# The first six scan units of the next item set beside the last sums, gating, out projection and norm of the item before

## The chip, the core and the metric

The kernel runs on one core of one Trainium2 chip. The metric is the device time of one execution in microseconds (us), as the median of several runs. The engines are TensorE (PE in the rows, with PEld its weight loads), VectorE (DVE), ScalarE (ACT), GpSimd (POOL) and SyncE (SP, here a DMA queue).

## What is computed

Eight items of 256 tokens and 256 features go through one block each. It is an FFN with 32 experts (the six best by a router, plus a shared part), then a Mamba mixer followed by a gated MLP, then the FFN again:

```python
x = x + 0.5 * ffn(layernorm(x))
h = layernorm(x)                               # attn's own input
h = h + mamba_mixer(rmsnorm(h, ln1_w))         # scan over 256 tokens, 512 channels, 16 states
x = x + h + mlp(rmsnorm(h, ln2_w))             # 1024 hidden
x = x + 0.5 * ffn(layernorm(x))

# the mixer's recurrence, for each token
hstate = exp(dt * A) * hstate + (dt * x) * B
y = sum over the 16 states of (hstate * C), + x * D_param, times silu(z), then out_proj
```

Everything is computed in float32 accuracy; the FFN's up and gate weights are split into a high and a low part and multiplied in three matmuls.

## The kernel before

The work is a pipeline over steps `t` = -1 to 9. Step `t` runs the first FFN of item `t` or a later one and the second FFN of an earlier item together, the mixer of item `t - 1`, and the MLP of item `t - 2`. In steps 1 and 3 to 7 the FFN handles two items at once (512 columns, the "full steps"), in the others one (256 columns).

`items_of(t)` writes the order of each step as one list of named pieces, and each engine walks that list and does its part of each piece, waiting on semaphores. So each engine is in order, and the list sets what stands beside what. In a step there are two lists that are merged:

- **heavy**: the MLP's 8 chunks (`gum`: gate and up, `down`), then the FFN's 26 chunks (`g`, `u`: six matmuls each; `by_g`: a VectorE product; `by_u`, `by_comb`: GpSimd products; `down`). The last six pieces (`TAIL`) follow the merge.
- **light**: the mixer. The 32 scan units of the item (`ub`: TensorE spreads B into a bank and VectorE multiplies it by `dtx`; `unit`: VectorE scans, TensorE spreads C, VectorE multiplies by it, GpSimd adds), with `front(1, "own")` (the second half of the projections) and the first norm and routing among the first 16, and `front(0, "next")` (the first half of the next item's projections), the norms before it and another routing among the last 16. Then the item's end: `yz` 3 (gating of the last quarter), `outp` (out projection on TensorE, after which VectorE adds it to `hn` and `res`), and `norm("rms2")`, whose result the next step's first `gum` needs.

`merge` gives each list a length by the table `WEIGHT`, scales both to 1, and sorts. The pieces of the item's end have large weights there, and so has what follows unit 31 (8): the light list is stretched at its end:

```python
    light += merge(unit_items(1), follow, SPACE) if follow else unit_items(1)
    light += [("yz", JC - 1), ("outp",)] + norm("rms2")
```

Step 2 differs: its mixer also does the norms and `front(0, "own")` of its item before unit 0 (`late_front`). Steps 7 and 8 differ too (`own`): after the MLP stands a serial chain, layernorm, router, eight dependent routing pieces and the split of the FFN's input (`hx`), before the first FFN chunk of the step can begin; about two thirds of the first half's units are merged with the MLP and this chain.

Small TensorE results go through three PSUM banks, `side0` to `side2`, in turn. A fill waits until the fill three before it has been used up: the bank of an `ub` is free when its unit has been scanned (line 1271), the bank of a `unit` when it has been multiplied (1277), that of `outp` when both additions (1289, 1290) are done. `near` pulls the closing piece of a bank forward when two other fills have come in between, and `late_order` lets VectorE and GpSimd do some pieces (`unit`: one, `outp`: four, `nm`: three) that many pieces later than the others. The scan writes to a ring of three buffers, which GpSimd's additions (1394, 1397) set free; the last additions of a quarter (1400, 1403) come before its `yz` (1282).

## Time and profile before

| | |
|---|---|
| median of 3 runs | 1793.54 us (1791.44 to 1796.31) |
| profiled execution | 1797.3 us, its span 1795.5 us |
| TensorE, matmuls | 1556.8 us busy (87%) |
| VectorE | 1288.6 us busy (72%) |
| GpSimd | 993.8 us busy (55%) |
| ScalarE | 842.9 us busy (47%) |
| step 2 (one item, late front) | 214.4 us |
| steps 3 to 6 (full) | 198.4, 199.7, 198.4 and 198.9 us |
| step 7 (full, with the serial chain) | 213.1 us |
| step 8 (one item, with the serial chain) | 156.9 us |

A step is taken here from the end of the last FFN `down` matmul of one step to that of the next. The steps follow each other on every engine, so the steps' lengths add up to the span. A busy time is the union of an engine's instructions; TensorE's matmuls overlap, and their busy time holds some of their waiting.

### The profile page before, as it was taken

How to read it: one execution, taken by the hardware profiler on the slowest of the kernel's cores; microseconds unless marked ns; L12 is line 12 of the kernel's file. 1: busy time of each engine (PE TensorE's matmuls, PEld its weight loads, DVE VectorE, ACT ScalarE, POOL GpSimd, SP SyncE). 2: the span in 40 equal slices, each digit the busy share in tenths (PEclk: the TensorE clock that was granted, in tenths of full speed). 3: DMA queues.
4: the chain of work that ended last, by engine and by line, in shares of the span. 5: the costliest groups of instructions: out<-in, count | busy, mean ns of one | idle time of the engine just before them, and what ended most of it. 6: DMA issues, size and time to landing. Idle time of an engine off the chain costs nothing. (4 is left out here: it accounts for less than half of the span.)

```text
span 1795.5 us, 22504 instructions
## 1 busy us (share of the span) xinstructions
PE 1556.8 (87%) x7088; PEld 1136.3 (63%) x7088; DVE 1288.6 (72%) x2085; ACT 842.9 (47%) x1676; POOL 993.8 (55%) x1048
## 2 busy tenths in 40 slices
PE   6878888777788999899998999899985999868979
PEld 5756555655676666666666666666663666647868
DVE  4536995478968878687959887887857776679421
ACT  4434543545624563356534663456433553445323
POOL 2523676345545766376646666476633766348525
PEclk9989999978989999999999999999996999979989
DMA  6863223332332323242333223232321332224434
GB/s 220 318 206 98 78 82 101 96 100 85 101 105 90 115 84 110 70 138 78 111 102 118 83 90 112 85 129 84 105 79 41 123 100 102 82 86 158 145 104 147
DMA packets 72278, 200.25 MB, mean 112 GB/s; under 512 B 9921, under 2 KB 22433, under 8 KB 71777
## 3 DMA queue, kind: packets, MB, share of 16 engines
q1 hardware_dynamic: 63968, 173.65, 29.1%
q0 software_dynamic: 8192, 25.17, 4.8%
q8 instruction: 57, 0.93, 0.2%
q14 instruction: 61, 0.49, 0.1%
HBM read 173.62 MB, written 23.59 MB: 110 GB/s over the span
## 5 line engine op out<-in xcount | busy, mean ns | idle before, releaser
L737 PE MATMUL gub<-x_hi,wr 128*128 128x512 f32 (+1 forms) x1040 | 425.4, 409 | 50.6 <-DVE hid L1107 44.8
L1397 POOL TENSOR_TENSOR ring<-ring 128x512 f32<-128x512 f32 x192 | 253.6, 1321 | 307.4 <-DVE ring L1277 306.2
L1376 POOL TENSOR_TENSOR hid<-hid,u_sb 128x512 f32<-128x512 f32 (+1 forms) x260 | 289.6, 1114 | 236.1 <-ACT u_sb L970 199.0
L818 PE MATMUL acc<-hid,w_down 128*128 128x512 f32 (+1 forms) x1040 | 408.9, 519 | 1.8 <-POOL hid L1376 1.8
L739 PE MATMUL gub<-x_hi,wr 128*128 128x512 f32 (+1 forms) x1040 | 370.8, 357 | 0.0
L738 PE MATMUL gub<-x_lo,wr 128*128 128x512 f32 (+1 forms) x1040 | 370.2, 356 | 0.0
L1271 DVE TENSOR_TENSOR_SCAN ring<-decays,side 128x512 f32<-128x512 f32 x256 | 310.5, 1213 | 28.9 <-ACT decays L1069 24.6
L970 ACT ACTIVATE u_sb<-gub 128x512 f32<-128x512 f32 (+1 forms) x260 | 132.7, 510 | 347.3 <-PE gub L739 346.8
L980 ACT ACTIVATE hid<-gub 128x256 f32<-128x256 f32 (+1 forms) x324 | 156.8, 484 | 278.2 <-PE gub L739 153.7
L1384 POOL TENSOR_TENSOR hid<-hid,weight 128x512 f32<-128x512 f32 (+1 forms) x240 | 272.9, 1137 | 15.8
L737 PEld LDWEIGHTS gub<-x_hi,wr 128*128 128x128 f32 x1040 | 205.4, 197 | 93.6 <-issue 58.1
L818 PEld LDWEIGHTS acc<-hid,w_down 128*128 128x128 f32 x1040 | 189.2, 197 | 97.2 <-issue 80.8
L1069 ACT ACTIVATE decays<-dts,a_neg 128x255 f32<-128x255 f32 x512 | 228.8, 497 | 3.8 <-DVE ring L1271 3.6
L1262 DVE TENSOR_TENSOR side<-dtx,side 128x512 f32<-128x512 f32 x256 | 176.8, 690 | 69.0 <-PE side L912 68.3
L739 PEld LDWEIGHTS gub<-x_hi,wr 128*128 128x128 f32 x1040 | 204.6, 197 | 27.1
L738 PEld LDWEIGHTS gub<-x_lo,wr 128*128 128x128 f32 x1040 | 205.8, 198 | 24.4 <-issue 5.5
L1107 DVE SCALAR_TENSOR_TENSOR hid<-hid,gub 128x512 f32<-128x512 f32 (+1 forms) x260 | 149.0, 573 | 98.3 <-ACT hid L980 98.3
L1277 DVE TENSOR_TENSOR ring<-ring,side 128x512 f32<-128x512 f32 x256 | 176.0, 687 | 59.5 <-PE side L915 36.2
L885 PE MATMUL side<-rn,w_in 128*128 128x256 f32 x448 | 120.4, 417 | 18.7 <-DVE ring L1271 13.5
L912 PE MATMUL side<-bst,sel_b 96*128 96x256 bf16 x512 | 103.7, 285 | 33.9 <-DVE ring L1271 18.1
L915 PE MATMUL side<-cst,sel_c 96*128 96x256 bf16 x512 | 103.9, 286 | 33.2 <-DVE ring L1271 32.7
L779 PE MATMUL gub<-xn_mlp,wm_gu 128*128 128x256 f32 x512 | 122.4, 387 | 0.0
(120 smaller groups left out, 1823.3 us busy)
## 6 DMA issues: line engine op xcount, KB each, us to landing
wr<-w_halves SPq DMA_DIRECT2D x234, 512.0 KB, 3.3
wm_gu<-in_w_mlp POOLq DMA_DIRECT2D x64, 256.0 KB, 3.1
w_halves<-wr SPq DMA_DIRECT2D x26, 512.0 KB, 4.9
wm_down<-in_w_mlp POOLq DMA_DIRECT2D x64, 128.0 KB, 2.6
w_raw<-in_w_gu SPq DMA_DIRECT2D x26, 256.0 KB, 4.3
rows<-parts SPq DMA_DIRECT2D x16, 384.0 KB, 2.3
cst<-rows SPq DMA_DIRECT2D x48, 128.0 KB, 2.6
xin<-in_x SPq DMA_DIRECT2D x8, 256.0 KB, 2.9
```

Source lines behind the costliest of these rows:

```text
L737: mm(out, w[:, 0, half, k, :], x_hi[:, k, a:b], start=(k == 0), stop=False)
L738: mm(out, w[:, 0, half, k, :], x_lo[:, k, a:b], start=False, stop=False)
L739: last = mm(out, w[:, 1, half, k, :], x_hi[:, k, a:b], start=False, stop=(k == KC - 1))
L818: last = mm(acc[k][:, a:b], w, h[:, a:b], start=(c == 0), stop=(c == (MLP_CHUNKS if mlp else FFN_CHUNKS) - 1))
L980: A(hid[c % HSLOTS][:, a:b], s.gub_of(it)[:, a:b], ACT.Tanh, scale=0.5).then_inc(sem["tanh_done"], 1)
L1069: A(decay[u % 2][:, h, 1:SEQ], dts[:, j, 1:SEQ], ACT.Exp, scale=a_neg[:, j, n:n + 1]).then_inc(sem["decay"], 1)
L1262: v.tensor_tensor(b, twice(dtx[:, j, :]), b, ALU.mult).then_inc(sem["driven"], 1)
L1271: v.tensor_tensor_scan(w.rearrange("p h s -> p (h s)"), decay[u % 2][:, :, :].rearrange("p h s -> p (h s)"), s.side_of(("ub", u))[:, :], 0 ...
L1277: v.tensor_tensor(w, w, pair(s.side_of(it)), ALU.mult).then_inc(sem["read_out"], 1)
L1376: nc.gpsimd.tensor_tensor(h, h, u_sb[c % USLOTS][:, a:b], ALU.mult).then_inc(sem["hidden"], 1)
L1384: nc.gpsimd.tensor_tensor(h, h, weight[c // 3 % CSLOTS][:, a:b], ALU.mult).then_inc(sem["weighted"], 1)
L1397: add(ysum, ysum, ring[:, u % 3], ALU.add).then_inc(sem["y_sum"], 1)
```

## The change

`LEAD = 6` units of an item are moved from the beginning of its step to the end of the step before. There they are merged, by the table `SPACE`, with the end of the item before (`yz` 3, `outp`, `rms2`). Steps 2 to 7 have such an end; steps 3 to 8 begin with unit 6. In steps 2 to 7 the extra weights of the item's end and after unit 31 are gone; they are kept as `ENDING` for steps 1 and 8, whose end nothing shares. The two additions behind the out projection become a piece of their own, `om`, so that other pieces can stand between; and the units carry their item's number, from which the ring's place and the scan's wait for a free buffer are worked out across items. The number of FFN columns in each step is as it was.

```diff
+LEAD = 6
...
-    "outp": {"side_filled": 1, "mixed": 2},
+    "outp": {"side_filled": 1},
+    "om": {"mixed": 2},
...
+def ring_at(unit):
+
+    return (unit[2] * UNITS + unit[1]) % 3
+
+
+def sums_of(u):
+    return {0: 0, PAIRS - 1: 3}.get(u % PAIRS, 1)
...
-    begin = len(light)
-    light += merge(unit_items(0), front(1, "own") + ln1, SPACE)
-    light += merge(unit_items(1), follow, SPACE) if follow else unit_items(1)
-    light += [("yz", JC - 1), ("outp",)] + norm("rms2")
+    begun = merge(unit_items(t - 1, 0 if late_front else LEAD, UNITS // 2), front(1, "own") + ln1, SPACE)
+    light += begun
+    units = unit_items(t - 1, UNITS // 2, UNITS)
+    light += merge(units, follow, SPACE) if follow else units
+    last = [("yz", JC - 1), ("outp",), ("om",)] + norm("rms2")
+    light += merge(unit_items(t, 0, LEAD), last, SPACE) if next_front else last
+    weight = WEIGHT if next_front else ENDING
...
-        cut = begin + len(unit_items(0) + front(1, "own")) * 2 // 3
-        out = hand + keep + merge(chain, light[:cut], WEIGHT) + merge(ff[:-TAIL], light[cut:], WEIGHT) + ff[-TAIL:]
+        cut = len(begun) * 2 // 3
+        out = hand + keep + merge(chain, light[:cut], weight) + merge(ff[:-TAIL], light[cut:], weight) + ff[-TAIL:]
...
-          "ub": 2, "unit": 2, ("unit", UNITS - 1): 8, "rt1": 1, "yz": 0.4,
-          ("yz", JC - 1): 3, "outp": 3, ("n1", "rms2"): 3, ("n2", "rms2"): 3, ("nm", "rms2"): 2,
+          "ub": 2, "unit": 2, "rt1": 1, "yz": 0.4, "outp": 0.5, "om": 1.6,
...
-         "yz": 0.1}
+         "yz": 0.1, "outp": 4, "om": 2, ("yz", JC - 1): 2, ("n1", "rms2"): 2}
+
+ENDING = {**WEIGHT, ("unit", UNITS - 1, BATCH - 1): 8, ("unit", UNITS - 1, 0): 8, ("yz", JC - 1): 3, "outp": 3, ("n1", "rms2"): 3,
+          ("n2", "rms2"): 3, ("nm", "rms2"): 2}
...
-       "xm": 0, "z": 0, "zm": 0, "dt": 0, "sp": 1, "sp_dt": 0, "sp_x": 0, "y0": 0, "ub": 0, "unit": 1, "rt1": 0, "outp": 4,
+       "xm": 0, "z": 0, "zm": 0, "dt": 0, "sp": 1, "sp_dt": 0, "sp_x": 0, "y0": 0, "ub": 0, "unit": 1, "rt1": 0, "outp": 0, "om": 0,
...
-                    w = ring[:, u % 3, :, :]
-                    dve.wait_ge(sem["decay"], s.count("decay", ("ub", u), 2))
-                    dve.wait_ge(sem["driven"], s.count("driven", ("ub", u), 1))
-                    if u >= 3:
-                        by = u - 3 if (u - 3) % PAIRS else u - 2
-                        dve.wait_ge(sem["y_sum"], s.count("y_sum", ("unit", by), 1))
+                    ub = ("ub",) + it[1:]
+                    w = ring[:, ring_at(it), :, :]
+                    dve.wait_ge(sem["decay"], s.count("decay", ub, 2))
+                    dve.wait_ge(sem["driven"], s.count("driven", ub, 1))
+
+                    free = u - 3 if (u - 3) % PAIRS else u - 2
+                    still = sum(sums_of(x) for x in range(free + 1, u)) + sums_of(free) - 1
+                    if (least := s.count("y_sum", it, 0, back=still)) is not None:
+                        dve.wait_ge(sem["y_sum"], least)
```

What this does to the engines' order is shown at three places. Line numbers of the changed kernel are up to 20 higher (818 is 835 there, 1271 is 1291).

VectorE at the end of step 4, before: from `y0` of the next item (`xs`) over the gating (`yg`) and the additions behind the out projection (`hn`, `res`) to the step's last additions (`x1_next`):

```order
L1253 TENSOR_SCALAR xs<-xs,vecs 128x256 x2
L1282 TENSOR_TENSOR yg<-xs,z2 128x256
L1107 SCALAR_TENSOR_TENSOR hid0<-hid0,gub1 128x512
L1289 SCALAR_TENSOR_TENSOR hn<-side0,hn 128x512
L1290 SCALAR_TENSOR_TENSOR res<-side0,res 128x512
L1107 SCALAR_TENSOR_TENSOR hid1<-hid1,gub0 128x512
L1172 SCALAR_TENSOR_TENSOR xn_mlp<-hn,lnw,rstd 128x256 x2
L1133 SCALAR_TENSOR_TENSOR x1_next<-acc0,x1_next 128x256
```

The same place after, from the gating on (the scan is printed as a SCALAR_TENSOR_TENSOR that writes `ring`):

```order
L1302 TENSOR_TENSOR yg<-xs,z2 128x256
L1291 SCALAR_TENSOR_TENSOR ring<-decays,side0 128x512
L1297 TENSOR_TENSOR ring<-ring,side1 128x512
L1279 TENSOR_TENSOR side0<-dtx,side0 128x512
L1124 SCALAR_TENSOR_TENSOR hid2<-hid2,gub0 128x512
L1291 SCALAR_TENSOR_TENSOR ring<-decays,side0 128x512
L1297 TENSOR_TENSOR ring<-ring,side1 128x512
L1309 SCALAR_TENSOR_TENSOR hn<-side2,hn 128x512
L1310 SCALAR_TENSOR_TENSOR res<-side2,res 128x512
L1279 TENSOR_TENSOR side2<-dtx,side2 128x512
L1124 SCALAR_TENSOR_TENSOR hid3<-hid3,gub2 128x512
L1291 SCALAR_TENSOR_TENSOR ring<-decays,side2 128x512
```

Between the gating and the additions behind the out projection stood one FFN product (`hid`). Now the scans and products of units 0 and 1 stand there, with unit 1's first product (1279) and one `hid`; four more units follow.

TensorE at the same place before, from the last FFN `down` ahead of the out projection (`yg,w_out`):

```order
L818 MATMUL acc0<-hid1,w_down 128x512
L818 MATMUL acc1<-hid1,w_down 128x512
L925 MATMUL side0<-yg,w_out 128x256 x8
L737 MATMUL gub2<-x_hi,wr0 128x512
L738 MATMUL gub2<-x_lo,wr0 128x512
```

And after, from the out projection to the fill that takes its bank, `side2`, again (`bst,sel_b` fills for `ub`, `cst,sel_c` for `unit`):

```order
L942 MATMUL side2<-yg,w_out 128x256 x8
L929 MATMUL side0<-bst,sel_b 128x256 x2
L835 MATMUL acc0<-hid3,w_down 128x512
L835 MATMUL acc1<-hid3,w_down 128x512
L932 MATMUL side1<-cst,sel_c 128x256 x2
L754 MATMUL gub1<-x_hi,wr4 128x512
L755 MATMUL gub1<-x_lo,wr4 128x512
L756 MATMUL gub1<-x_hi,wr4 128x512
L754 MATMUL gub1<-x_hi,wr4 128x512
L755 MATMUL gub1<-x_lo,wr4 128x512
L756 MATMUL gub1<-x_hi,wr4 128x512
L929 MATMUL side2<-bst,sel_b 128x256 x2
```

The out projection's bank used to be taken by nothing in the step's last chunks; now it is wanted again after one `down`, two small fills and one FFN half.

TensorE at the start of step 5, before, from the first `ub` (`wm_gu`, `wm_down` are the MLP, `rn,w_in` and `dtr,w_dt` the projections of `front(1)`):

```order
L912 MATMUL side2<-bst,sel_b 128x256 x2
L885 MATMUL side0<-rn,w_in 128x256 x4
L779 MATMUL gub0<-xn_mlp,wm_gu0 128x256 x4
L915 MATMUL side1<-cst,sel_c 128x256 x2
L896 MATMUL side2<-dtr,w_dt 128x256 x2
L912 MATMUL side0<-bst,sel_b 128x256 x2
L818 MATMUL acc0<-hid1,wm_down1 128x256
L818 MATMUL acc1<-hid1,wm_down1 128x256
L915 MATMUL side1<-cst,sel_c 128x256 x2
```

And after:

```order
L929 MATMUL side2<-bst,sel_b 128x256 x2
L902 MATMUL side0<-rn,w_in 128x256 x4
L796 MATMUL gub0<-xn_mlp,wm_gu0 128x256 x4
L913 MATMUL side1<-dtr,w_dt 128x256 x2
L932 MATMUL side2<-cst,sel_c 128x256 x2
L835 MATMUL acc0<-hid1,wm_down1 128x256
L835 MATMUL acc1<-hid1,wm_down1 128x256
L929 MATMUL side0<-bst,sel_b 128x256 x2
```

The `dt` projection moved ahead of the first `unit` fill and out of the bank of the step's first `ub`; the `unit` fill has that bank now. By the end of the MLP part (the eighth `down`) TensorE has filled for units 6 to 10 instead of units 0 to 5 and the `ub` of 6.

## Rows read from the trace of the kernel before

**Rows 1.** The page's busy times, us and share of the span

```profile
PE 1556.8 (87%) x7088; PEld 1136.3 (63%) x7088; DVE 1288.6 (72%) x2085; ACT 842.9 (47%) x1676; POOL 993.8 (55%) x1048
```

**Rows 2.** Busy us by stretch: steps 2, 3, 4, 6, 7 and 8

```profile
core 0: us, PE busy (x) PEld busy (x) DVE busy (x) ACT busy (x) POOL busy (x), PEclk, DMA share, GB/s
313.30:527.70 214.40, 161.26 (x831) 132.89 (x829) 163.55 (x272) 104.72 (x218) 95.49 (x118) 0.87 0.31 98
527.70:726.10 198.40, 184.56 (x783) 126.28 (x781) 159.12 (x248) 101.28 (x191) 121.90 (x118) 0.99 0.30 98
726.10:925.80 199.70, 187.71 (x784) 128.25 (x782) 158.71 (x250) 101.39 (x191) 121.45 (x118) 0.97 0.31 100
1124.20:1323.10 198.90, 182.29 (x767) 123.87 (x764) 155.66 (x227) 97.79 (x185) 122.10 (x118) 0.99 0.31 99
1323.10:1536.20 213.10, 187.43 (x766) 127.85 (x764) 152.10 (x227) 97.66 (x185) 121.37 (x118) 0.94 0.28 91
1536.20:1693.10 156.90, 124.50 (x715) 103.60 (x715) 121.40 (x199) 67.35 (x158) 90.37 (x118) 0.89 0.36 117
```

**Rows 3.** The same for step 4's MLP part, its FFN body, its tail

```profile
726.10:766.40 40.30, 33.08 (x145) 26.13 (x143) 31.66 (x57) 15.00 (x32) 13.38 (x25) 0.88 0.21 65
766.40:906.00 139.60, 135.59 (x574) 90.03 (x572) 119.49 (x185) 79.45 (x149) 100.31 (x89) 1.00 0.35 113
906.00:925.80 19.80, 19.04 (x69) 12.09 (x68) 7.56 (x10) 6.93 (x10) 7.76 (x6) 1.00 0.24 79
```

**Rows 4.** Waits in step 4's MLP part: waiter, awaited, us in total, times, longest

```profile
PE side L885 <- DVE ring L1271: 3.4, 1, 3.4
...
PE side L896 <- DVE ring L1271: 2.4, 1, 2.4
...
PE side L915 <- DVE ring L1271: 1.3, 1, 1.3
```

**Rows 5.** Four lines' instructions: ns min/median/max, first and last start in us

```profile
L1262 DVE TENSOR_TENSOR side<-dtx,side x256: 675/691/697, 164.2 to 1670.7; 128x512 f32<-128x512 f32 x128
...
L1271 DVE TENSOR_TENSOR_SCAN ring<-decays,side x256: 1201/1212/1222, 165.0 to 1671.7; 128x512 f32<-128x512 f32 x128
...
L1277 DVE TENSOR_TENSOR ring<-ring,side x256: 686/687/691, 169.0 to 1673.0; 128x512 f32<-128x512 f32 x128
...
L1282 DVE TENSOR_TENSOR yg<-xs,z x32: 410/420/1511, 218.7 to 1677.4; 128x256 f32<-128x256 f32 x32
```

**Rows 6.** Timeline of PE, end of step 4: start, us, instruction, idle before

```profile
910.16 3.72 PE L925 MATMUL side<-yg,w_out 128*128 128x256 f32 x16 [0.76 <-DVE yg L1282]
...
913.53 0.58 PE L737 MATMUL gub<-x_hi,wr 128*128 128x512 f32 x1
...
916.46 1.13 PE L843 MATMUL side<-sq,mean_w 128*128 128x256 f32 x4
...
920.53 5.31 PE L818 MATMUL acc<-hid,w_down 128*128 128x512 f32 x12
```

**Rows 7.** The same of DVE, the addition behind the out projection

```profile
913.92 0.69 DVE L1289 SCALAR_TENSOR_TENSOR hn<-side,hn 128x512 f32<-128x512 f32 x1 [3.21 <-PE side L925]
```

**Rows 8.** Busy us by stretch: step 2's second half and its tail

```profile
393.00:513.00 120.00, 90.21 (x499) 73.29 (x498) 111.25 (x177) 61.85 (x136) 64.93 (x69) 0.89 0.30 99
513.00:527.70 14.70, 12.15 (x58) 10.35 (x59) 4.89 (x10) 4.91 (x8) 3.48 (x5) 0.88 0.30 96
```

**Rows 9.** The same for three parts of step 7, two of step 8

```profile
1323.10:1358.10 35.00, 27.75 (x141) 21.89 (x138) 29.75 (x54) 15.37 (x33) 14.12 (x25) 1.00 0.23 67
1358.10:1386.10 28.00, 11.34 (x40) 7.38 (x40) 20.41 (x45) 9.40 (x18) 9.68 (x17) 0.61 0.17 52
1386.10:1536.20 150.10, 148.34 (x587) 98.57 (x586) 101.94 (x130) 72.89 (x135) 97.57 (x76) 0.98 0.31 104
...
1572.60:1599.90 27.30, 11.47 (x41) 7.57 (x41) 19.91 (x45) 10.25 (x19) 10.07 (x17) 0.63 0.15 44
1599.90:1674.00 74.10, 64.44 (x434) 55.72 (x433) 67.73 (x96) 35.36 (x94) 56.65 (x64) 0.96 0.49 160
```

More of the change, by code:

```diff
@@ L153, in routing, with unit_items @@
     return [("rt1", call)] + [("rq", call, i) for i in range(len(ROUTE))]
-def unit_items(half):
+def unit_items(item, begin, end):
     out = []
-    for u in range(half * UNITS // 2, (half + 1) * UNITS // 2):
+    for u in range(begin, end):
         j, p = u // PAIRS, u % PAIRS
-        out += [("ub", u), ("unit", u)]
+        out += [("ub", u, item), ("unit", u, item)]
         out += [("yz", j - 1)] if p == 2 and j else []
@@ L186 @@
 FILLS = ("n1", "n2", "rt1", "rt2", "z", "x", "split", "dt", "ub", "unit", "outp")
-ENDS = {"ub": "unit", "z": "zm", "split": "sr", "n1": "nc"}
+ENDS = {"ub": "unit", "outp": "om", "z": "zm", "split": "sr", "n1": "nc"}
 def near(items):
@@ L253, in items_of @@
     if not mlp:
-        out = hand + keep + merge(ff[:-TAIL], light, WEIGHT) + ahead + ff[-TAIL:]
+        out = hand + keep + merge(ff[:-TAIL], light, weight) + ahead + ff[-TAIL:]
     elif own:
         chain = mlp_items() + ahead + norm("ln2a") + routing("f1") + [("rt2", "f1"), ("hx", "f1")]
-        cut = begin + len(unit_items(0) + front(1, "own")) * 2 // 3
-        out = hand + keep + merge(chain, light[:cut], WEIGHT) + merge(ff[:-TAIL], light[cut:], WEIGHT) + ff[-TAIL:]
+        cut = len(begun) * 2 // 3
+        out = hand + keep + merge(chain, light[:cut], weight) + merge(ff[:-TAIL], light[cut:], weight) + ff[-TAIL:]
     else:
         heavy = mlp_items() + ahead + ff
-        out = hand + heavy[:6] + keep + merge(heavy[6:-TAIL], light, WEIGHT) + heavy[-TAIL:]
+        out = hand + heavy[:6] + keep + merge(heavy[6:-TAIL], light, weight) + heavy[-TAIL:]
     out = near(after(out, turn, *turns))
@@ L265, in items_of @@
         at = out.index
-        assert at(("shift",)) < at(("n1", "lnA")) and at(("ub", UNITS // 2)) < at(("split", 0, "next"))
+        assert at(("shift",)) < at(("n1", "lnA")) and at(("ub", UNITS // 2, t - 1)) < at(("split", 0, "next"))
         assert at(("yz", 1)) < min(at(("xc", 0, "next", 0)), at(("z", 0, "next")))
@@ L395 @@
 }
-ENDED_BY = {"g": "by_g", "ub": "unit", "z": "zm", "split": "sr", "n1": "nc"}
+ENDED_BY = {"g": "by_g", "ub": "unit", "outp": "om", "z": "zm", "split": "sr", "n1": "nc"}
 BANKS = {"side": SIDES, "gub": GUBS}
@@ L990, in do @@
                     else:
-                        act.wait_ge(sem["mixed"], s.count("mixed", ("outp",), 1))
+                        act.wait_ge(sem["mixed"], s.count("mixed", ("om",), 1))
                     A(sq[:], src[:], ACT.Square).then_inc(sem["squared"], 1)
@@ L1279, in do @@
                     j = it[1]
-                    dve.wait_ge(sem["y_sum"], s.count("y_sum", ("unit", PAIRS * j + PAIRS - 1), 3))
+                    dve.wait_ge(sem["y_sum"], s.count("y_sum", ("unit", PAIRS * j + PAIRS - 1, s.t() - 1), 3))
                     dve.wait_ge(sem["z_done"], s.count("z_done", it, 0))
                     v.tensor_tensor(yg[:, j], y[:, j], z2[:, j], ALU.mult).then_inc(sem["y_gated"], 1)
-                elif kind == "outp":
-                    dve.wait_ge(sem["side_filled"], s.count("side_filled", it, 1))
+                elif kind == "om":
+                    dve.wait_ge(sem["side_filled"], s.count("side_filled", ("outp",), 1))
                     dve.wait_ge(sem["r_base"], s.count("r_base", ("r0",), 1))
                     dve.wait_ge(sem["carried"], s.count("carried", ("carry",), 1))
-                    b = pair(s.side_of(it))
+                    b = pair(s.side_of(("outp",)))
                     v.scalar_tensor_tensor(hn[:], b, 0.5, hn[:], ALU.mult, ALU.add).then_inc(sem["mixed"], 1)
@@ L1393, in do @@
                             pool.wait_ge(sem["y_sum"], least)
-                        add(ysum, ring[:, (u - 1) % 3], ring[:, u % 3], ALU.add).then_inc(sem["y_sum"], 1)
+                        add(ysum, ring[:, ring_at(("unit", u - 1, it[2]))], ring[:, ring_at(it)], ALU.add).then_inc(sem["y_sum"], 1)
                     else:
                         pool.wait_ge(sem["y_sum"], s.count("y_sum", it, 0))
-                        add(ysum, ysum, ring[:, u % 3], ALU.add).then_inc(sem["y_sum"], 1)
+                        add(ysum, ysum, ring[:, ring_at(it)], ALU.add).then_inc(sem["y_sum"], 1)
                     if p == PAIRS - 1:
```

2 lines of the change are left out of this document (1 added, 1 removed).

## The prediction

> **What bounds the kernel now.** Begin with the page's busy times: the matmuls take 87% of the span and VectorE 72% [rows 1]. Neither number says which engine ends a wait in a given stretch, so the next view is the busy time by step [rows 2]. The full steps are TensorE's: steps 3 and 4 have TensorE busy for 184.6 and 187.7 us of 198.4 and 199.7, VectorE for 159. Step 2 and step 8 are different. In step 2 TensorE is busy for only 161.3 us of 214.4, in step 8 for 124.5 of 156.9, and both have VectorE at 163.6 and 121.4.
>
> Then cut a full step into three [rows 3]. Step 4's last 19.8 us are the item's end: TensorE is busy for 19.0 of them, VectorE for 7.6. This is the hole into which the change puts units. But TensorE is full there, so filling it gives nothing by itself. What can be gained is where TensorE waits, and that is the MLP part: 40.3 us with TensorE busy for 33.1, at a granted clock of 0.88, while the 139.6 us of FFN body have 135.6 busy at 1.00. The waits of that part name three fills that waited for a scan, 3.4, 2.4 and 1.3 us [rows 4]; they are the whole 7.2 us of idle time. So the chain there is TensorE, fill, VectorE's scan, next fill; less scan work in it should help.
>
> In step 2's second half VectorE is busy for 111.3 of 120.0 us, and for only 4.9 of the last 14.7 [rows 8]. Steps 7 and 8 have the serial routing chain: in step 7 the 35.0 us of MLP and 28.0 of chain hold 27.8 and 11.3 us of matmuls and 29.8 and 20.4 us of VectorE, and the FFN part after them is TensorE's (148.3 of 150.1). In step 8 the FFN part is VectorE's: 67.7 of 74.1 us [rows 9].
>
> **The price of a unit.** On VectorE 0.69 + 1.21 + 0.69 = 2.59 us [rows 5], so the six lead units are 15.5 us of VectorE's time. No unit is added or removed in all; each step from 3 to 7 gets six at its end and loses six at its start, step 2 only gets, step 8 only loses. The counts of DMAs and of SyncE's waits don't change; the DMAs that bring B and C for unit 0 are issued some three FFN chunks ahead of it as now placed, and a chunk takes over 5 us, so I cost them at nothing (if that cover were gone, one landing would stand in the open in each of six steps).
>
> **Step 2.** 15.5 us of VectorE work comes in. The tail has 14.7 - 4.9 = 9.8 us of idle VectorE time [rows 8], and I let 8 of it be filled, since part of it lies before the first unit can start or behind the last. The rest lengthens the step: +7.5 us. Bounds: +5.7 (all filled) and +15.5 (none).
>
> **Steps 3 to 5.** In the MLP part TensorE now fills for units 6 to 10 instead of units 0 to 5 and the first product of unit 6. On VectorE this is 5 x 2.59 = 13.0 instead of 6 x 2.59 + 0.69 = 16.2 us, so 3.2 less. In their place two more pieces of the projections' second half come forward, but to the part's end, behind what TensorE waits for there. Beside it, the `dt` projection, which waited 2.4 us for the first scan [rows 4], has a free bank now; the next fill waits for the same scan instead, so only `dt`'s own matmuls are won, some 0.5 us. Sum: -3.7.
>
> At the tail something new is queued. The third lead unit's first fill takes the out projection's bank, `side2`, and must wait for both additions behind it. From the out projection's end TensorE has one `down` (5.31 / 12 x 4 = 1.8 us), one FFN half ((916.46 - 913.53) / 2 = 1.5) and two small fills (0.4 by my estimate) to do, 3.7 in all [rows 6]. VectorE has unit 1's first product, an FFN product of that kind, the scan, the product and the two additions: 0.69 + 0.7 + 1.21 + 0.69 + 2 x 0.69 = 4.7 us [rows 5, 7]. So TensorE stops for about 1 us (with a little for the order, 1.2), and behind it in its queue stand the last FFN chunks. VectorE's own wait for the out projection, 3.2 us now [rows 7], is filled by unit 0, which helps nobody. Net -2.5 us a step, -7.5 for three. Bounds for a step: -7.2 (all idle time of the MLP part gone) and +3 (nothing gained there, three times the tail stop).
>
> **Step 6.** The same, with a little more slack in it (16.6 us without a matmul against 12.0 in step 4, [rows 2]): -3.
>
> **Step 7.** Before the FFN's first chunk VectorE had ten whole units to do, now six: 4 x 2.59 = 10.4 us less in 63.0 us. But VectorE was already idle for 12.9 of them [rows 9], waiting for the chain of small steps, so I count half: -5. The FFN part is TensorE's and gets the fills of five more units: 20 matmuls, at most 0.23 each by the out projection's records [rows 6], so 0 to 4.6, and I take +2. Net -3.
>
> **Step 8.** The same -5 at the start (27.3 us of chain with 19.9 of VectorE, [rows 9]). In the part where VectorE is the limit one unit fewer remains, -2.6, and I round to -3. Net -8.
>
> **Steps 1 and 9** keep their content; in step 1 the additions only move by a place or two: 0.
>
> Sum: +7.5 - 7.5 - 3 - 3 - 8 = **-14 us**. Against the profiled execution's 1797.3 that is 1783.3; the median of the runs is 3.8 us lower, so 1793.5 - 14 = 1779.5.
>
> **A rule weighed against the trace.** The gating (1282) stands between the last sum and the out projection, and it takes 0.41 us at least, 0.42 at the median, but 1.51 at the longest, while the three instructions of a unit never vary by more than 0.02 us [rows 5]. The Trainium skill, SBUF — State Buffer, "SBUF: two separate sides", says that VectorE and GpSimd share one port pair under an exclusive lock, taken by a VectorE instruction with two SBUF inputs, and that the loser blocks for a whole instruction of the other. The rows agree: the gating has two SBUF inputs, the unit's instructions take one of theirs from PSUM. By this rule the units themselves cost their 2.59 us beside any GpSimd work. But GpSimd gets their additions in the tail, and the gating could more often meet one.
>
> **The rivals.**
> - *More is won* (1760). The waits of the MLP part go altogether, and the clock with them: 7.2 us idle and a clock of 0.88 in 40.3 us [rows 3]. Another 5 us in each of steps 3 to 6: -34. For it: all of the idle time there is waiting for scans. Against it: the first unit of the step still meets the same chain of fill, product, scan.
> - *The units only change places* (1793). The full steps stay as they are, since TensorE is busy for 94% of them and VectorE's hole was never in the way; step 2 costs its 7.5 and step 8 gives its 8. For it: the tail's 19.0 of 19.8 us. Against it: the 7.2 us.
> - *The gating is blocked in the tail* (1786). 1.51 - 0.41 = 1.1 us in each of the six tails, +6.6: 1793.5 - 14 + 6.6. For it: the longest 1282. Against it: the median is the free value, beside a GpSimd that is busy for 122 of 200 us. It is the lock rule's case.
> - *Slower: TensorE stops in the tail* (1800 and more). The last sum, gating, out projection, additions and the next fill of `side2` are one chain through three engines, with units now queued ahead of its VectorE pieces. Each microsecond costs six times. I have 1.2 in the sum; with s instead the sum is -14 + 6 (s - 1.2), which is nothing at s = 3.5 and +6.4 at 4.6, a stop as long as all of VectorE's work in that piece. For it: the fill really is behind both additions. Against it: TensorE's 3.7 us of other work ahead of it.
>
> **How the numbers follow.** About 0.3% (5.4 us) is what a measurement of this kernel can tell. Chances: forecast 0.50 (1771 to 1787), more 0.17, change of places 0.12, gating 0.08, slower 0.13. The predicted time is the forecast's, 1779.5. The range leaves out the slower case and a little of "more": 1761 to 1795. Faster by over 0.3% (under 1788.2): 0.50 + 0.17 + most of the gating's, 0.06 = 0.73. Within 0.3%: 0.14. Slower: 0.13.
>
> **What would show it.** Step 2 some 7.5 us longer with VectorE busy over 170 us, and its tail no longer empty; the MLP part of steps 3 to 5 near 37 us with the waits for 1291 (the scan) under 4 us; in the tail one wait of a `side` fill for `res` (1310) of about 1 us; step 7 near 210 and step 8 near 149 us. The prediction is wrong if the full steps don't get shorter, if the MLP part keeps its 40 us, or if the tail grows beyond 21 us. It is too timid if the granted clock in the MLP part rises to 1.00.

## The result, and the profile after

The changed kernel takes 1802.8 us (median of 4 runs, 1801.5 to 1805.2), where the kernel before took 1793.3 beside it: a ratio of 1.0053, 95% interval 1.0035 to 1.0071. It is slower by 0.5%. The forecast was 14 us faster and its range ended at 1795.

The page's busy times (first line below) hardly differ from [rows 1]: no work was added. The second fence has the busy times of steps 2, 3, 4, 6, 7 and 8, columns as in [rows 2].

```profile
PE 1555.1 (86%) x7088; PEld 1136.0 (63%) x7088; DVE 1292.4 (72%) x2085; ACT 843.6 (47%) x1676; POOL 991.2 (55%) x1048
```

```profile
309.40:540.10 230.70, 168.09 (x853) 137.40 (x852) 177.53 (x289) 109.69 (x230) 100.16 (x123) 0.86 0.28 91
540.10:744.90 204.80, 188.56 (x784) 128.87 (x783) 160.88 (x248) 101.79 (x191) 121.20 (x118) 0.97 0.29 94
744.90:945.80 200.90, 184.67 (x783) 125.95 (x782) 160.95 (x250) 101.79 (x191) 121.51 (x118) 0.99 0.31 99
1147.30:1347.00 199.70, 183.77 (x767) 125.53 (x765) 152.60 (x227) 96.52 (x185) 122.53 (x118) 0.97 0.30 99
1347.00:1553.70 206.70, 188.03 (x765) 128.81 (x764) 152.61 (x227) 97.49 (x185) 120.95 (x118) 0.93 0.29 94
1553.70:1696.70 143.00, 116.81 (x692) 99.57 (x691) 106.52 (x181) 62.75 (x146) 84.69 (x113) 0.92 0.39 128
```

Against [rows 2], step by step: step 2 is 16.3 us longer, steps 3, 4 and 5 together 10.6, step 6 0.8; step 7 is 6.4 shorter, step 8 13.9. Steps 0, 1 and 9 differ by -3.0 together. That is the span's +4.5. In step 2 VectorE is busy 14.0 us more (163.6 to 177.5) and the step is 16.3 longer: none of the idle time that VectorE had there was filled. The step is as long as before up to the start of the out projection (202.4 us against 201.3); from there to the step's end it went from 13.2 to 28.3 us, and VectorE's idle time there from 9.8 to 11.0 (before, then after):

```profile
514.55:527.70 13.15, 12.15 (x58) 10.35 (x59) 3.34 (x7) 4.91 (x8) 2.01 (x3) 0.87 0.33 107
511.83:540.10 28.27, 21.16 (x97) 16.97 (x98) 17.28 (x24) 8.95 (x18) 10.37 (x11) 0.80 0.22 70
```

The next fence cuts step 4 into MLP part, FFN body and last 34.9 us, to be held against [rows 3], and adds the last 35.1 us of step 2.

```profile
744.90:779.50 34.60, 28.53 (x141) 23.15 (x140) 28.72 (x54) 14.85 (x31) 13.16 (x25) 1.00 0.24 76
779.50:910.90 131.40, 125.42 (x522) 83.68 (x520) 109.71 (x168) 73.74 (x137) 88.86 (x78) 0.99 0.34 112
910.90:945.80 34.90, 30.72 (x122) 19.12 (x122) 22.52 (x30) 13.20 (x24) 19.49 (x16) 1.00 0.23 76
505.00:540.10 35.10, 22.27 (x105) 17.86 (x106) 23.91 (x35) 10.23 (x22) 14.08 (x15) 0.82 0.22 71
```

The MLP part went from 40.3 to 34.6 us. Everything behind it in the step went from 159.4 to 166.3. The gain of the MLP part is mostly not the one that was forecast: its waits for the scan fell only from 7.1 us [rows 4] to 5.9, and the rest is that TensorE was busy for 28.5 us instead of 33.1, with four matmuls fewer and at a granted clock of 1.00 instead of 0.88. In step 3 the clock of that part went the other way, from 0.96 to 0.90, and the part only from 39.5 to 38.4 us. The waits behind it are among TensorE's waits of the whole of step 4 (waiter, awaited, us in total, times, longest):

```profile
PE side L860 <- ACT sq L1009: 4.3, 1, 4.3
PE side L932 <- DVE ring L1291: 2.5, 3, 1.7
PE side L902 <- DVE ring L1291: 2.3, 1, 2.3
PE side L942 <- DVE yg L1302: 1.8, 1, 1.8
PE side L929 <- DVE ring L1291: 1.4, 1, 1.4
PE acc L835 <- POOL hid L1396: 1.2, 1, 1.2
PE side L929 <- DVE res L1310: 1.2, 1, 1.2
```

Only the waits for the scan (1291) and the old wait for the gating (1302, 0.76 us in [rows 6]) have a counterpart before. Three are new: 4.3 us for the squares of a norm (the first of the FFN part) at 51 us into the step, 1.2 us for the additions behind the out projection, and 1.2 us for a GpSimd product in the step's last piece. The timeline of the trace shows these, and the larger ones of step 2's tail (start, us, instruction, idle before it and what ended it):

```profile
505.86 0.39 PE L932 MATMUL side<-cst,sel_c 96*128 96x256 bf16 x2 [1.18 <-DVE ring L1291]
511.83 6.25 PE L942 MATMUL side<-yg,w_out 128*128 128x256 f32 x16 [4.86 <-DVE yg L1302]
522.38 0.39 PE L929 MATMUL side<-bst,sel_b 96*128 96x256 bf16 x2 [3.00 <-DVE res L1310]
538.01 2.07 PE L835 MATMUL acc<-hid,w_down 128*128 128x256 f32 x4 [4.11 <-POOL hid L1396]
...
796.24 1.06 PE L860 MATMUL side<-sq,mean_w 128*128 128x256 f32 x3 [4.28 <-ACT sq L1009]
...
914.45 3.72 PE L942 MATMUL side<-yg,w_out 128*128 128x256 f32 x16 [1.75 <-DVE yg L1302]
...
922.89 0.39 PE L929 MATMUL side<-bst,sel_b 96*128 96x256 bf16 x2 [1.20 <-DVE res L1310]
...
943.85 1.98 PE L835 MATMUL acc<-hid,w_down 128*128 128x512 f32 x4 [1.23 <-POOL hid L1396]
```

Three things are to be read there. In step 2's tail the stops add up to 13.2 us; but the step's tail before had 3.84 us of waiting for the gating and 1.00 for the GpSimd product already, so what is new is 1.0 for the gating, 3.0 for the additions, 3.1 for GpSimd and the first 1.2. The norm that is waited for stood 65 us into step 4 before (791.54) and nothing waited for it; the merge now puts it at 51. By then VectorE has 11 us less work behind it, but it is wanted 14 us earlier, and from 778.65 to the instruction that feeds the squares (794.84) VectorE goes from one instruction to the next (step 4 from its start to that norm, before and after):

```profile
726.10:791.50 65.40, 57.98 (x255) 43.56 (x253) 55.23 (x90) 29.05 (x60) 35.51 (x51) 0.92 0.36 112
744.90:796.20 51.30, 40.99 (x198) 32.18 (x196) 44.23 (x75) 22.38 (x46) 26.59 (x44) 1.00 0.36 111
```

And the out projection starts 31.4 us before the end of step 4 (914.45 against 945.8), where it used to start 15.6 us before it (910.16 in [rows 6], end 925.8): with six units merged beside it, the whole of the item's own work has to be done earlier in the step.

The last wait is a queue of GpSimd. Its timeline at the end of step 4:

```profile
941.31 1.26 POOL L1417 TENSOR_TENSOR ring<-ring 128x512 f32<-128x512 f32 x1 [3.71 <-DVE ring L1297]
942.53 1.26 POOL L1396 TENSOR_TENSOR hid<-hid,u_sb 128x512 f32<-128x512 f32 x1
```

GpSimd stands idle for 3.71 us until unit 5's product is there, adds it, and only then makes the product that the last `down` waits for. The addition is ahead of it in GpSimd's order; e5 below tests whether it is what holds the product up.

### The profile page after: what moved, and what is told of

It reads as the page before. It is cut to its first block and busy times, and to the rows that moved or that the text cites. A ratio compares the mean times of both kernels' runs of the same rounds, so it can differ in the third digit from the quotient of the medians.

```text
span 1800.0 us, 22495 instructions
## 1 busy us (share of the span) xinstructions
PE 1555.1 (86%) x7088; PEld 1136.0 (63%) x7088; DVE 1292.4 (72%) x2085; ACT 843.6 (47%) x1676; POOL 991.2 (55%) x1048
## 5 line engine op out<-in xcount | busy, mean ns | idle before, releaser
L1404 POOL TENSOR_TENSOR hid<-hid,weight 128x512 f32<-128x512 f32 (+1 forms) x240 | 269.0, 1121 | 14.8
L1086 ACT ACTIVATE decays<-dts,a_neg 128x255 f32<-128x255 f32 x512 | 228.9, 497 | 6.1 <-DVE ring L1291 6.0
L756 PEld LDWEIGHTS gub<-x_hi,wr 128*128 128x128 f32 x1040 | 204.3, 196 | 27.9
```

The lines of the kernel that those rows point to most:

```text
L756: last = mm(out, w[:, 1, half, k, :], x_hi[:, k, a:b], start=False, stop=(k == KC - 1))
L1086: A(decay[u % 2][:, h, 1:SEQ], dts[:, j, 1:SEQ], ACT.Exp, scale=a_neg[:, j, n:n + 1]).then_inc(sem["decay"], 1)
L1404: nc.gpsimd.tensor_tensor(h, h, weight[c // 3 % CSLOTS][:, a:b], ALU.mult).then_inc(sem["weighted"], 1)
```

## The experiments

All run on one core, each timed beside the kernel before; each ratio is to that. "Gives" is a step that starts with unit 6, "receives" one that has the next item's first units at its end.

| kernel | what differs from the changed kernel | us | ratio, 95% |
|---|---|---|---|
| e1 | step 2 doesn't receive | 1792.9 | 0.9994 [0.9983, 1.0004] |
| e2 | only step 7 receives | 1784.2 | 0.9953 [0.9937, 0.9969] |
| e3 | no step receives | 1795.4 | 1.0009 [0.9998, 1.0020] |
| e4 | variance and routing fills of `ln1` later | 1801.8 | 1.0039 [1.0025, 1.0053] |
| e5 | unit 5 behind GpSimd's last product | 1794.2 | 0.9998 [0.9987, 1.0008] |
| e6 | e5, and all leads behind the out projection | 1813.4 | 1.0111 [1.0095, 1.0127] |
| e7 | e5, light work spaced by VectorE time | 1803.1 | 1.0058 [1.0042, 1.0074] |
| e8 | three units instead of six | 1805.3 | 1.0069 [1.0050, 1.0088] |
| e9 | e2, additions at the out projection in steps that don't receive | 1787.0 | 0.9957 [0.9941, 0.9974] |
| e10 | e9 with seven units | 1779.7 | 0.9916 [0.9895, 0.9937] |
| e11 | as e9, but only step 2 receives | 1813.0 | 1.0100 [1.0078, 1.0122] |
| e12 | as e9, but steps 6 and 7 receive | 1781.1 | 0.9934 [0.9911, 0.9956] |
| e13 | e7, one VectorE product moved | 1800.6 | 1.0040 [1.0026, 1.0053] |
| e14 | e11, the same product moved | 1811.8 | 1.0099 [1.0081, 1.0117] |
| e15 | e12 with seven units | 1774.5 | 0.9898 [0.9883, 0.9913] |
| e16 | e12 with six and seven units | 1776.5 | 0.9898 [0.9885, 0.9911] |

**Who pays and who gains: e1, e2, e3.** One table of leads (here e1's; `{7: 6}` in e2, `{}` in e3) replaces the constant:

```diff
-LEAD = 6
+LEADS = {i: 6 for i in range(3, 8)}
...
-    light += merge(unit_items(t, 0, LEAD), last, SPACE) if next_front else last
-    weight = WEIGHT if next_front else ENDING
+    leads = unit_items(t, 0, LEADS.get(t, 0))
+    light += merge(leads, last, SPACE) if leads else last
+    weight = WEIGHT if leads else ENDING
```

> Step 2 keeps all its work; the leads begin with item 3, in step 3's tail, so that step 3 holds 38 units and steps 4 to 8 begin with unit 6. Theory A (the change lost in step 2, which has no room for six units, and a few us at each tail): step 2 returns from 230.7 to about 214 us, step 3 to about 203 (from 204.8), the others stay, so about 1786 us. Theory B (VectorE's work is the limit wherever it stands): the 15.5 us reappear in step 3, which goes to 215 or more, about 1799 us.

> Leads for the last item alone, in step 7's tail; all steps before it as in the kernel before. Theory A (each step that only receives six units pays some 16 us, each that only gives wins some 14, and a step that does both is unchanged): step 7 rises from 213.1 to 225 or more, since it receives and doesn't give, step 8 falls from 156.9 to 143, the sum is 1793 to 1797 us. Theory B (a full step with a VectorE hole in its tail takes six units for nearly nothing, and the loss was step 2's alone): step 7 stays under 218, the sum is 1785 us or less.

> No leads anywhere, the large weights at every item's end, but the additions behind the out projection still a piece of their own, which VectorE meets directly instead of four pieces late. If only the moved units matter: 1793 us as before, within 0.3%. If the separate additions cost or give something by themselves (TensorE or VectorE waiting at the item's end): up to 2 us a step, 1783 to 1805 us.

In e1 step 2 is back at 213.1 us, but step 3, which now receives and doesn't give, takes 215.8, 17.3 more than before. Its busy times, and its longest waits of TensorE:

```profile
519.40:735.20 215.80, 192.39 (x809) 131.03 (x807) 176.68 (x266) 106.27 (x203) 127.56 (x123) 0.97 0.27 90
```

```profile
PE side L933 <- DVE ring L1292: 5.3, 2, 4.7
PE gub L755 <- DVE hid L1125: 3.9, 3, 1.7
PE side L943 <- DVE yg L1303: 3.6, 1, 3.6
```

The total, 1792.9, lies between the two theories, and step 3 is as theory B had it: the price belongs to whichever step receives without giving. Against the changed kernel e1 has step 2 17.6 us shorter and step 3 11.0 longer, and is 10 us faster in the median. e2 moves the price to step 7: 216.0 us, only 2.9 more than before, and step 8 takes 143.9, 13 less. In e3, without any leads, the new separate piece for the additions alone changes nothing that can be measured.

**GpSimd's queue: e5.**

```diff
+    if next_front:
+        out.remove(("unit", LEAD - 1, t))
+        out.insert(out.index(("by_u", "ff", FFN_CHUNKS - 1)) + 1, ("unit", LEAD - 1, t))
     out = near(after(out, turn, *turns))
```

> The changed kernel, but unit 5 of the next item stands behind the step's last GpSimd product, so that its addition no longer lies ahead of that product in GpSimd's queue. If the queue is the cause of the wait of the last downs (4.1 us in step 2, 1.2 in the full steps): 4 us less in step 2 and 1 in each full step, 8 us in all, about 1795 us. If the last product is late for another reason: no change, 1803 us.

The time falls from 1802.8 to 1794.2, which is that of the kernel before. In step 2 the edit changes GpSimd's order alone; in steps 3 to 6 TensorE's too. The wait of 4.1 us at the end of step 2 is 0.7, and step 2 is 3.2 us shorter (227.5); the 1.2 us at the end of the full steps are gone. Step 3 is 5.0 us shorter: 1.5 at its end and 3.6 in its MLP part. Its first 24 matmuls took 7.4 us in the changed kernel, right behind the stop of 4.1, where those of step 4 took 5.4; the granted clock up to the end of the first `down` was 0.75, and it is 1.00 in e5. Steps 4 and 5 are no shorter in the profiles (201.2 and 201.1 us against 200.9 and 201.4), so what the 1.2 us of a full step are worth by themselves is not shown. One piece in the wrong place of one queue was thus worth most of the change's loss (8.6 of 9.5 us); without it the change is worth nothing.

**The order in the tail and in the start: e4, e6, e7.**

In e4, in steps 3 to 5 (the condition holds in these alone):

```diff
+        for it, behind in ((("n2", "ln1"), ("down", "ff", 0)), (("rt1", "f1"), ("down", "ff", 1))):
+            out.remove(it)
+            out.insert(out.index(behind) + 1, it)
```

In e6, with e5's edit:

```diff
-    light += merge(unit_items(t, 0, LEAD), last, SPACE) if next_front else last
+    light += last[:2] + merge(unit_items(t, 0, LEAD), last[2:], SPACE) if next_front else last
```

In e7, with e5's edit, weights for steps 3 to 7 that follow VectorE's time for each piece:

```diff
+EVEN = {**WEIGHT, "ub": 1, "unit": 1.6, "xc": 2.6, "sp": 2.0, "sp_dt": 1.9, "sp_x": 1.0, "y0": 1.8, "sr": 0.6, "rq": 0.7}
```

> The changed kernel, but in steps 3 to 5 the variance matmul of ln1 stands one FFN half and one down later, and the router matmul behind the next down. Theory A (the 4.3 us wait for the square is a cost of the order): it goes to about 1 us in three steps, 8 to 10 us less, about 1793 us. Theory B (VectorE is behind after the MLP part, and TensorE meets it somewhere): the wait moves to the next fill or gate, less than 3 us won, 1800 to 1803 us.

> The kernel with unit 5 behind GpSimd's last product (1794.2 us), and with all six lead units behind the out projection, so that VectorE's first lead product is not ahead of the gating and two units are not ahead of the additions. Theory A (the tail's waits for the gating, 1.8 us, and for the additions, 1.2, come from what is queued ahead of them, and are worth their size): 1.5 to 3 us less in each of steps 2 to 7, so 1777 to 1785 us. Theory B (VectorE's order only decides where TensorE meets it): under 1 us a step, 1789 to 1794 us.

> The kernel with unit 5 behind GpSimd's last product (1794.2 us), and in steps 3 to 7 the weights of the merge changed so that the light list is spaced by VectorE's time (units less, convolution and first product more): some 2 us of VectorE's work move from the first six FFN chunks and the MLP part to later ones. If TensorE's 4.3 us wait at the variance matmul of ln1 is VectorE's backlog at the start of the step: 2 us less in each of steps 3 to 5 and about as much in 6 and 7, 1784 to 1788 us. If the backlog isn't the cause: 1793 to 1796 us.

e4 took the wait of 4.3 us for the squares away, and the waits for the FFN product `hid` went from 0.9 to 4.0: the same lateness of VectorE, met by another reader; nothing was gained that can be told. In e6 the wait for the gating rose from 1.8 to 3.7 us in steps 3 to 5 and the total by 19 us over e5 (8 of them in step 7): that the waits of the tail come from the units queued ahead of the gating was wrong. In e7 the waits for `hid` rose to 6.3 us a step and the total by 9 over e5: that the light work was spaced badly for VectorE was wrong as I had it.

**Fewer units: e8** (`LEAD = 3`).

> The changed kernel with three lead units instead of six (and GpSimd's queue as in the changed kernel). If all costs and gains go with the number of units: half of the way from 1793.3 to 1802.8, 1798 us; step 2 about 222 us, step 8 about 150. If the tail's waits come with the first lead unit (its queueing ahead of the gating, the out projection's bank and the last GpSimd product): step 2 stays above 224, 1800 to 1806 us.

Neither theory holds. Step 2 takes 214.0 us: three units do fit into the hole. But steps 3 to 5 take 204.2 to 205.3 us, 7.6 more together than with six, while step 6 is 3 us shorter (196.4), and step 8 only loses 4.0. So the cost of a full step doesn't go with the number of units; the places into which the pieces fall count for 2 to 3 us a step.

**Giving and receiving priced apart: e9, e11, e12, e10, e15, e16.** In these the weight of `om` in `ENDING` is 0, so steps that neither give nor receive have the order of before.

> Leads for the last item alone (step 7 receives, step 8 gives), and in the other steps both additions stand at the out projection as in the kernel before, so steps 1 to 6 have its order. Theory (the total is what the receiving step pays less what the last giving step wins, and nothing else): step 7 about 215 us (+2 to +3 against before), step 8 about 143 (-13 to -14), total 1782 to 1784, ratio 0.994. If e2's ratio owed something to its changed places of the additions in steps 1 to 6, this one is not better than 1788; if these places cost e2 something (the separate additions with no leads seemed to cost 2 us a step in 3 to 5), this one is under 1781.

> Leads for item 2 alone: step 2 receives six units, step 3 gives and receives none, all other steps have the order of before. This prices what a full step wins when it only gives. Theory A (a full step is TensorE's, and VectorE's load sets its start, so a step that only gives has 15.5 us less for VectorE and loses the waits of its MLP part: 7.2 us of idle and the lower clock): step 3 at 190 to 193 us against 198.5, step 2 at 228 to 231, total +8 to +11, about 1803. Theory B (a full step wins nothing by giving, since TensorE sets it): step 3 at 197 to 199, total +14 to +16, about 1808.

> Leads for the last two items: step 6 only receives, step 7 receives and gives, step 8 only gives; steps 1 to 5 as before. Theory (each step that does both is about as long as before, so the cost moves to whichever step only receives): step 7 at 207 (-6), step 8 at 143 (-14), step 6 +11 to +17 since it is a full step whose VectorE has only its tail free; total 1784 to 1790. Rival (step 6 has more room than a full step: 16.6 us without a matmul): step 6 +5 or less, total 1779 or less, better than e9.

| step | neither | receives | gives | both |
|---|---|---|---|---|
| 2 | 214.4 | 228.9 (e11) | | |
| 3 | 198.4 | 215.8 (e1) | 201.8 (e11), 198.9 (e14, below) | 199.8 to 204.8 |
| 6 | 198.9 | 206.3 (e12) | | 199.2 to 200.2 |
| 7 | 213.1 | 216.6 (e9) | | 206.6 (e12) |
| 8 | 156.9 | | 144.8 (e9), 142.5 (e12) | |

A full step wins nothing by giving six units away: in e11 step 3 is 3.4 us longer than before, though its MLP part shrank from 39.5 us to 34.2 (538.5 to 572.7 in its trace). Theory A of that run fell. Of theory B the outcome holds, with a loss on top (1813 us instead of 1808), but not its reason: TensorE stands idle for 15.9 us of that step, and for 13.8 before, so it is not TensorE's work that fills it; the waits move from the MLP part to later places. A step that receives pays 14.5 us at step 2, 17.3 at step 3, 7.4 at step 6 and 3.5 at step 7. e9's total is 3 us above what was expected, with step 7 at 216.6 and step 8 at 144.8; in e12 step 6's price lies between what its theory and its rival had. Only steps 7 and 8, which have the serial chain, win by giving: 10 and 12 to 14 us. The total is the price of the first step that receives and what the full steps behind it lose (0 to 6 us each), less these two. That is why leads for all items come out at nothing or worse, and leads for the last two are 12 us faster.

> As the kernel of e9 (leads for the last item alone), with seven leads instead of six. Theory (step 7's FFN part has room on VectorE: 102 of 150 us busy): step 7 within 1 us of e9's, step 8 one more unit shorter, 141 to 142, so 1 to 2 us under e9's time. Rival (six fill the room, TensorE sets that part and gets four more small matmuls, about 1 us): the same as e9 within 1 us. If the time is above e9's by 2 us or more, the seventh unit meets the step's last FFN chunks as unit 5 met GpSimd's queue.

> Leads for the last two items as in e12, with seven units in both instead of six. Theory (step 7 and 8 win with each unit more, since step 8 went from 144.8 to 137.5 with the seventh; step 6 only receives and has VectorE room in its tail for about six): step 6 208 to 210, step 7 205 to 207, step 8 137 to 138, total 1774 to 1779. Rival (the seventh unit in a full step meets GpSimd's queue or a full TensorE): step 6 above 212 or step 7 above 209, total 1781 or more.

> As e12 (leads for the last two items), with six units in step 6 and seven in step 7. Theory (the seventh unit's gain is in step 8 alone, 142.5 to about 137.5, and costs step 7 about 2): total 1776 to 1779. Rival: step 8's seventh unit won by chance of its order, and the total stays at 1780 to 1783.

The seventh unit pays more than I expected (e10 is 7.3 us under e9 in the median, expected were 1 to 2): step 8 falls to 137.5 us in all three. The rows of e15 are steps 6, 7 and 8:

```profile
1122.70:1328.80 206.10, 187.43 (x796) 125.97 (x793) 172.97 (x248) 102.99 (x199) 129.56 (x124) 0.98 0.30 96
1328.80:1535.60 206.80, 187.47 (x766) 127.69 (x764) 151.52 (x228) 97.27 (x185) 121.22 (x118) 0.93 0.29 94
1535.60:1673.00 137.40, 117.49 (x687) 100.86 (x686) 101.91 (x177) 62.19 (x144) 82.43 (x112) 0.89 0.42 133
```

e15 is the fastest kernel of this study, 1774.5 us, 18 us under the kernel before (16 to 21). e16 can't be told from it.

**VectorE locked out: e13, e14.** The 6.3 us of waiting for `hid` in e7 are in each of steps 3 to 5 a stop of 4.44 us (last row) and small ones. VectorE's timeline before it, and GpSimd's:

```profile
785.76 0.69 DVE L1301 TENSOR_TENSOR ring<-ring,side 128x512 f32<-128x512 f32 x1
786.37 0.68 DVE L1128 SCALAR_TENSOR_TENSOR hid<-hid,gub 128x512 f32<-128x512 f32 x1
786.97 5.27 DVE L1270 TENSOR_TENSOR dtx<-dts,xs 128x512 f32<-128x512 f32 x1
792.27 1.23 DVE L1274 TENSOR_SCALAR xs<-xs,vecs 128x256 f32<-128x256 f32 x1
...
786.71 1.29 POOL L1400 TENSOR_TENSOR hid<-hid,u_sb 128x512 f32<-128x512 f32 x1
787.96 1.28 POOL L1421 TENSOR_TENSOR ring<-ring 128x512 f32<-128x512 f32 x1
789.20 1.26 POOL L1408 TENSOR_TENSOR hid<-hid,weight 128x512 f32<-128x512 f32 x1
790.43 1.25 POOL L1400 TENSOR_TENSOR hid<-hid,u_sb 128x512 f32<-128x512 f32 x1
791.76 1.60 POOL L1408 TENSOR_TENSOR hid<-hid,weight 128x512 f32<-128x512 f32 x1
...
794.51 0.77 PE L758 MATMUL gub<-x_hi,wr 128*128 128x512 f32 x1 [4.44 <-DVE hid L1128]
```

The product of `dts` and `xs`, both in SBUF, takes 5.27 us where its kind takes 0.68 at the median. It begins while GpSimd is in the first of four instructions that follow each other without a pause, and ends 0.5 us after GpSimd's first pause. In e11's step 3 the same product takes 5.05 us, and TensorE waits 4.84 us behind it. Both kernels put it at the same place, behind unit 11. e13 and e14 put it, with the pair of `xs` products behind it, behind unit 13:

```diff
+        moved = [("sp_x", 1, "own"), ("y0", 1, "own")]
+        out = [it for it in out if it not in moved]
+        at13 = out.index(("unit", 13, t - 1)) + 1
+        out[at13:at13] = moved
```

> As e7 (spaced-out order), but in steps 3, 4 and 5 the piece sp_x (one VectorE product, dtx from dts and xs, both in SBUF) and the y0 behind it stand two units later, away from GpSimd's run of four back-to-back instructions. Theory (VectorE is locked out by that run: 5.27 us instead of 0.68): the instruction is back under 2.1 us, the wait for hid falls by 3 to 4.6 us, and each of steps 3 to 5 is 3 to 4.6 us shorter, 9 to 14 in all, so 1789 to 1794 against e7's 1803. Rival (VectorE's backlog at the step's start is the cause, the long instruction only lies in it): the wait appears at another fill and the total stays at 1801 to 1804.

> As e11 (leads for item 2 alone), but in step 3 sp_x and y0 stand two units later. Theory (the lockout of 4.4 us by GpSimd's run made step 3's wait for hid of 4.8 us): step 3 at 197.5 to 199 us against 201.8, total 1809 to 1810. Rival (backlog): step 3 within 1 us of 201.8.

Its place is cured in both: no instruction of that kind takes over 1.76 us. In e14 step 3 fell from 201.8 to 198.9 us, within what the theory had, though 0.6 us of that lies in the MLP part, ahead of the moved pieces, and one profile can't tell 2.9 us for certain; the total fell by 1.2, which that run can't tell from nothing. In e13 the waits for `hid` fell from 6.3 to 1.9, but the steps stayed at 204.3 to 204.5 and the total fell by 2.5 instead of 9 to 14. The timelines of e13 show what came instead:

```profile
795.63 0.69 DVE L1275 TENSOR_TENSOR dtx<-dts,xs 128x512 f32<-128x512 f32 x1
796.35 2.50 DVE L1279 TENSOR_SCALAR xs<-xs,vecs 128x256 f32<-128x256 f32 x2
798.78 0.68 DVE L1202 TENSOR_TENSOR xc_f<-xc_f,rstd 128x512 f32<-128x512 f32 x1
...
799.51 0.85 PE L882 MATMUL side<-w_router,xc_f 128*128 128x32 f32 x3 [3.81 <-DVE xc_f L1202]
```

The moved pieces now stand directly ahead of the norm's last product, for which TensorE waits 3.81 us; 3.2 us of that is the three moved instructions. The same wait, 3.7 us, is in e14's step 3. So the lockout is real and was paid by TensorE, but e13 exchanged it for another late piece, and whether its absence is worth the expected 9 us is not shown.

## Why the prediction was wrong

Each step of it, against the traces:

- **Step 2, +7.5.** It is +16.3, over my upper bound of 15.5. The step that failed is "the tail has 9.8 us of idle VectorE time, and I let 8 of it be filled". VectorE was idle 50.9 us in step 2 before and is idle 53.2 now. The idle time of the old tail was room for three units (e8: step 2 as long as before), not for six. The gating, out projection and additions are a chain through three engines. With six units beside it TensorE waits 13.2 us in the tail where it waited 4.8, the out projection runs at a lower clock, and VectorE waits as long for the first fill behind it (4.64 us) as it used to for the out projection (5.14). That these delays make up the loss is argued from the trace; only GpSimd's part was taken away alone (e5: 3.2 us of the step).
- **Steps 3 to 5, MLP part -3.7.** In step 4 it was -5.7 (40.3 to 34.6), but that the number came near was luck: the waits for the scan, which the term was about, fell by 1.2 us and stayed at 5.9, where I had put under 4. The rest came with one unit's fills less and mostly with the clock, from 0.88 to 1.00 in that part. In step 3 the part gave only 1.1.
- **Steps 3 to 5, net -2.5 each.** Wrong: +10.6 for the three. I carried the MLP part's gain through to the step's end, since TensorE was busy for 135.6 of 139.6 us of the body. But VectorE's lateness only moved: 4.3 us at the first norm of the FFN part (and when that was moved, 4.0 us for `hid`, e4). I had priced the six units less as VectorE time won and left out that the merge moves all other light pieces forward too, that norm by 14 us. e11 isolates it: six units fewer for VectorE, a shorter MLP part, and no shorter step. That the full steps win nothing my own rival "the units only change places" said, though for another reason.
- **The tail stop at `side2`, 1.2.** It is 1.20 us in step 4, 1.5 at other full steps of other kernels, and 3.00 in step 2.
- **GpSimd in the tail.** I counted GpSimd's additions only as a partner for the lock, not as a queue ahead of the last `by_u`. It is 1.2 us of waiting in a full step and 3.1 more than before in step 2, and the clock at the start of step 3 with it; e5 recovers 8.6 us of the median in all, of the 23 between forecast and result. It stood in the order: the piece list had unit 5 ahead of the last FFN product.
- **Step 6, -3:** +0.8. **Step 7, -3:** -6.4, and **step 8, -8:** -13.9. Both of the last were mis-sized by halving what VectorE saves ahead of the first FFN chunk. From the start of step 7 to its first FFN matmul, before and after:

```profile
1323.10:1386.90 63.80, 39.87 (x183) 29.48 (x180) 50.95 (x99) 25.23 (x51) 23.80 (x42) 0.82 0.20 60
1347.00:1402.60 55.60, 38.24 (x163) 29.66 (x161) 41.93 (x86) 21.76 (x43) 20.42 (x39) 0.80 0.23 68
```

  That is -8.2 where I had -5; the rest of step 7 went from 149.3 to 151.1 us, close to the +2 that I had for it. In step 8 the same stretch went from 64.4 to 54.9 us, -9.5 for -5, and the rest from 92.5 to 88.1, -4.4 for -3. VectorE's work in step 7's stretch fell by 9.0 us and its idle time stayed (12.9 and 13.7 us), so nearly all of the saving came off the stretch, and not half.
- **The gating rival.** Not what happened: 1302's longest is 1.50 us, as before, though its median rose from 0.42 to 0.51.

```profile
L1302 DVE TENSOR_TENSOR yg<-xs,z x32: 409/512/1500, 218.4 to 1680.5; 128x256 f32<-128x256 f32 x32
```

- **The slower rival** (TensorE stops in the tail, 0.13) has the right sign, but not the right size or mechanism. The new stops of step 4's tail are 1.2 + 1.2 + 1.0 = 3.4 us; its formula gives -14 + 6 (3.4 - 1.2) = -1 us. The rest lies in step 2 and at the start of the full steps.

What stays open: no run puts that norm back to its old place with the units gone, so that its earlier place makes VectorE 4 us late is read from the trace and not tested. e4 and e13 show that the lateness passes from one reader to the next when one is moved. Nor is it shown why step 6 pays 7.4 us for receiving and step 3 17.3.

## What to carry to other kernels

Idle time of an engine at the end of a stage is room only as far as no chain through that engine is what the others are waiting for (here it held three units and not six); count how often the new pieces stand ahead of one that is awaited, in every in-order queue, also that of the engine with the least to do. When work is passed from each stage to the one before, the inner stages come out nearly even, and the whole is the price at the first that only receives against the gain at the last that only gives: price these two, and start the passing where it is cheap. A full step didn't get shorter here by what was taken off VectorE: where an order is made by merging two lists, fewer pieces in one move all the others forward, and what is waited for is wanted earlier too.

## What the runs showed of the hardware

- **One VectorE instruction waited for four of GpSimd's.** A product with both inputs in SBUF took 5.27 us instead of 0.68, through four back-to-back GpSimd instructions of 1.25 to 1.29 us, three times in e7; 5.05 us in e11. The Trainium skill, SBUF — State Buffer, "SBUF: two separate sides", has the loser of the lock blocked for the whole instruction that holds it, which is 1.3 us here; by these rows the block can last until the other engine pauses. It doesn't always: in other places the same engines changed over at the next boundary. Summed over the trace (each VectorE instruction's time above the tenth percentile of its kind, where that is over 0.15 us), such excess is 145.5 us before, 148.7 after, 163.6 in e7 and 152.0 in e13, 16 to 27 us of each full step in these traces; it counts every slow instruction, whether the lock is its reason or not. In the kernel before, one product took 2.84 us beside two GpSimd instructions.
- **A stop costs more than its own length.** The out projection, the same sixteen matmuls each time, took 3.72 us behind stops of 0.76 and 1.75 us (step 4, before and after), at a granted clock of 1.00; 5.38 us behind 3.84 (step 2 before), at 0.66; and 6.25 us behind 4.86 (step 2 after), at 0.58. The clock has two levels, 1.2 and 2.4 GHz, so part of the longer ones ran at the lower. The first 24 matmuls of step 3 took 7.4 us behind the stop of 4.1 and 5.4 in step 4.
- **The same list can take 5 us more.** Step 6 has one order in e12 and e16, and TensorE's waits add up to about the same, yet it took 206.3 and 211.2 us (e12 first):

```profile
1118.30:1324.60 206.30, 186.84 (x792) 125.61 (x789) 170.34 (x245) 101.78 (x197) 128.09 (x123) 0.98 0.29 95
```

```profile
1119.30:1330.50 211.20, 190.56 (x792) 127.80 (x790) 170.28 (x245) 101.76 (x197) 127.92 (x123) 0.97 0.29 93
```

  VectorE's busy time is the same; TensorE's is 3.7 us more for the same 792 matmuls. The difference lies in two stretches, in which the granted clock was 1.00 in e12 and 0.71 and 0.79 in e16; what decides that behind the same stops is not shown. A single step's length in one profile is thus good to some 5 us, so the medians decide, and of the prices above those under 5 us are not certain.
